# Edge sums of a graph network with the one-hots of half groups as the fixed operand, then copied, turned and added

## What is computed

```python
# layer 0: message = [nodes[src], edge] @ W, summed per receiver, then norm and a three-layer MLP
agg = segment_sum(concat([nodes[src], edge_attr_64], -1) @ W_message, dst)
h = layer_norm(relu(agg) + nodes);  nodes = layer_norm(nodes + relu_mlp_skip(h))
x = experts_0(x + ...)              # 16 experts, 2 of them per node
# layer 1: rows cut to their 32 largest entries, mean over the neighbours
x = x + segment_sum(sparse(x)[src], dst) / degree
x = experts_1(...)                  # 8 experts, 2 of them per node
```

## Time and profile before

| | us |
|---|---|
| median of 3 runs | 1449.61 (1449.51 to 1450.31) |
| span of the profiled execution | 1607.9 |
| setup | 0 to 40.6 |
| O0: groups, adjacency, node MLP | 40.6 to 558 |
| routing and experts of layer 0 | 558 to 865 |
| sparse rows | 865 to 1030 |
| O1: groups and neighbour means | 1030 to 1362 |
| routing, experts of layer 1, output | 1362 to 1608 |

### The profile page before, as it was taken

The page is one execution under the profiler, slowest core; times in us unless marked ns, Lnnn a source line. Parts: engine busy times, 40 slices in busy tenths (PEclk is TensorE's granted clock), DMA queues, the critical chain, the costliest instruction groups (busy, mean ns, idle before and its releaser), DMA issues. The chain is left out here.

```text
span 1607.9 us, 27179 instructions
## 1 busy us (share of the span) xinstructions
PE 1175.4 (73%) x7129; PEld 1007.4 (63%) x7130; DVE 709.5 (44%) x2376; ACT 661.1 (41%) x1842; POOL 746.3 (46%) x841
## 2 busy tenths in 40 slices
PE   1287788887899739999993777377778867478780
PEld 1277777876789628999992333166557666367670
DVE  7133455655446761111114999334433225522225
ACT  3554555654113333444443555576651002323230
POOL 5655555655550004222215776366456660266650
PEclk9977888877989958999996999755678885588885
DMA  5543344444440047999992232433223332422227
GB/s 173 147 112 107 107 109 115 118 114 105 112 115 25 17 160 254 350 352 352 349 322 85 85 89 72 132 90 95 76 76 103 97 94 70 133 78 78 81 75 249
DMA packets 186771, 220.03 MB, mean 137 GB/s; under 512 B 69103, under 2 KB 148503, under 8 KB 186382
## 3 DMA queue, kind: packets, MB, share of 16 engines
q1 hardware_dynamic: 148240, 125.81, 24.4%
q0 software_dynamic: 32352, 87.30, 18.7%
q10 hardware_dynamic: 6046, 5.40, 1.1%
HBM read 187.33 MB, written 32.19 MB: 137 GB/s over the span
## 5 line engine op out<-in xcount | busy, mean ns | idle before, releaser
L783 POOL DMA_INDIRECT O0G<-n_rows,src_tab x260 | 251.1, 966 | 194.5 <-PE O0ps_sums L802 91.8
L783 POOL DMA_INDIRECT O1G<-sparse_rows,src_tab x188 | 180.0, 958 | 125.9 <-issue 58.7
L802 PE MATMUL O0ps_sums<-O0OH,O0G 128*128 128x80 f32 x1040 | 160.1, 319 | 1.3 <-issue 1.2
L802 PEld LDWEIGHTS O0ps_sums<-O0OH,O0G 128*128 128x128 f32 x1040 | 153.7, 234 | 6.3 <-issue 2.7
L802 PEld LDWEIGHTS O1ps_sums<-O1OH,O1G 128*128 128x128 f32 x752 | 122.9, 251 | 14.1 <-issue 10.2
L1982 POOL DMA_INDIRECT e0xs<-token_rows,e0idx x60 | 56.8, 947 | 159.7 <-ACT e0idx L2071 155.9
L802 PE MATMUL O1ps_sums<-O1OH,O1G 128*128 128x80 f32 x752 | 123.3, 333 | 9.8 <-issue 7.4
L2027 PE MATMUL e0ps_h<-e0xT,e0W 128*128 128x128 f32 x1024 | 126.7, 277 | 0.8 <-ACT e0xT L2077 0.8
L2122 DVE TENSOR_TENSOR e0ys<-e0ps_y,NR 128x256 f32<-128x256 f32 x64 | 27.2, 425 | 215.3 <-PE e0ps_y L2041 215.3
L2027 PEld LDWEIGHTS e0ps_h<-e0xT,e0W 128*128 128x128 f32 x1024 | 121.1, 194 | 1.5 <-issue 1.4
L2041 PE MATMUL e0ps_y<-e0W,e0hidT 128*128 128x256 f32 x512 | 120.9, 379 | 0.0
(11 more groups left out here) (382 smaller groups left out, 2701.5 us busy)
## 6 DMA issues: line engine op xcount, KB each, us to landing
e0W<-in_L_ffn_w SPq DMA_DIRECT2D x128, 512.0 KB
O0EA<-in_edge_attr SPq DMA_DIRECT2D x97, 128.0 KB
expert_out<-e0ys SPq DMA_DIRECT2D x64, 128.0 KB
O0G<-n_rows,src_tab POOLq DMA_INDIRECT x260
e1W_all<-in_L_ffn_w SPq DMA_DIRECT2D x16, 256.0 KB, 6.0
n_rows<-NR SPq DMA_DIRECT2D x5, 640.0 KB
token_rows<-O0N SPq DMA_DIRECT2D x25, 128.0 KB
m0own<-token_rows SPq DMA_DIRECT2D x25, 128.0 KB
```

Of the source, the lines that this page charges most:

```text
L783: pool.indirect_dma_start(out=self.G[:, s, k, :], out_offset=None, in_=self.rows_dram, in_offset=bass.IndirectOffsetOnAxis(ap=src_tab[:, g ...
L802: last = nc.tensor.matmul(self.ps[o % 2][0:rows.shape[1], half * P:half * P + WINDOW], rows, self.OH[:, h, k, 0:WINDOW], start=(k == 0), s ...
```

## The change

The two operands of a gathered group's products change places. The one-hot of a tile (now 48 columns wide, relative to the base of its *half* group of two tiles) is the fixed operand; the gathered rows (256 columns) and the edge rows (65 columns) move. The first half's sums go to PSUM partitions 0 to 47, the second's to 64 to 111, in the order of tiles 0, 2, 1, 3. The result has nodes on the partitions, so it must be turned: ScalarE copies 112 x 321 (O1: 112 x 256) into SBUF (`copy`), TensorE turns it by three transposes (two in O1) into a third bank (`turn`, issued in the next slot before the products of the next group), and VectorE adds the two halves each at its own base (`add`, two value loads, two adds). Edges are dealt to tiles by 128 consecutive ones instead of every fourth, and the edge rows are loaded so too. Setup computes bases and relative places per half. To make room, the node stage's gate logits share a bank with another result (`ps_bg`, `ps_g`), with waits to match; small tables reuse `w_nodes` once it is no longer needed; `before` is made in `route`. The width of a group's window, which the order's safety limits use, goes from 80 to 88. The near groups and both adjacencies stay. Core of the diff:

```diff
-WINDOW = 80
+WINDOW = 88
+HALF_W = 48
+HALF_AT = 64
...
+rel_half = sb("rel_half", [P, NS, 2, GC // 2])
+base_half = sb("base_half", [1, NS, 2], I32)
...
-        for c in range(3):
-            last = nc.tensor.matmul(ps_e[0:1, c * P:c * P + NG], ends[:, c:c + 1], ident[0:NG, 0:NG], start=True, stop=True)
+        for c in range(5):
+            last = nc.tensor.matmul(ps_e[0:1, c * NG:(c + 1) * NG], ends[:, c:c + 1], ident[0:NG, 0:NG], start=True, stop=True)
         last.then_inc(s_rowp, 1)
         pe.wait_ge(s_row, 1)
-        nc.tensor.matmul(ps_b[:, 0:NG], ones[0:1, :], endr[0:1, 0, :], start=True, stop=True).then_inc(s_bb, 1)
+        nc.tensor.matmul(ps_b[:, 0:NG], ones[0:1, :], endr[0:1, 0, :], start=True, stop=True)
+        nc.tensor.matmul(ps_b[:, NG:3 * NG], ones[0:1, :], endr[0:1, 3:5, :].rearrange("a c g -> a (c g)"), start=True, stop=True).then_inc(s_bb, 1)
...
-                nc.vector.tensor_reduce(ends[:, 0:1], dlow[:], AX_X, ALU.min)
-                nc.vector.tensor_reduce(ends[:, 1:2], dstf[:], AX_X, ALU.max).then_inc(s_dv, 1)
+                nc.vector.tensor_reduce(ends[:, 3:5], dlow[:].rearrange("g (h e) -> g h e", h=2), AX_X, ALU.min)
+                nc.vector.tensor_reduce(half_top[:], dstf[:].rearrange("g (h e) -> g h e", h=2), AX_X, ALU.max).then_inc(s_dv, 1)
...
+                nc.vector.tensor_tensor(ends[:, 0:1], ends[:, 3:4], ends[:, 4:5], ALU.min)
+                nc.vector.tensor_tensor(half_span[:, 0, :], half_top[:], ends[:, 3:5], ALU.subtract).then_inc(s_dv, 1)
+                dve.wait_ge(s_dv, 6)
+                nc.vector.tensor_scalar(half_span[:, 1, :], ends[:, 3:5], ends[:, 0:1], float(2 * HALF_W - 1 - WINDOW), ALU.subtract, ALU.add).then_inc(s_dv, 1)
+                dve.wait_ge(s_dv, 7)
                 nc.vector.tensor_scalar(ends[:, 2:3], ends[:, 0:1], -1.0, MORE_TILE * P - 0.5, ALU.mult, ALU.add)
+                nc.vector.tensor_reduce(half_top[:, 0:1], half_span[:].rearrange("g k h -> g (k h)"), AX_X, ALU.max)
                 nc.vector.tensor_tensor(ends[:, 1:2], ends[:, 1:2], ends[:, 0:1], ALU.subtract).then_inc(s_dv, 1)
                 dve.wait_ge(s_dn, 5)
...
+        for h in range(2):
+            nc.vector.tensor_tensor(rel_half[:, :, h, :], rel_tab[:, DENSE_GROUPS:NG, 2 * h:2 * h + 2],
+                                    ps_b[:, (1 + h) * NG + DENSE_GROUPS:(2 + h) * NG].unsqueeze(2).to_broadcast([P, NS, 2]), ALU.subtract).then_inc(s_dv, 1)
...
+        hots, rows = HR * GC * HALF_W, 2 * self.row_cols
+        hot = sb(tag + "OH", [P, max(hots + rows, GU * GC * P)], F32, c)
+        self.OH = hot[:, 0:hots].rearrange("p (h c w) -> p h c w", h=HR, c=GC)
+        self.R = hot[:, hots:hots + rows].rearrange("p (r d) -> p r d", r=2)
         self.OH_any = hot[:, 0:GU * GC * P].rearrange("p (h c w) -> p h c w", h=GU, c=GC)
         self.ps = [pb(f"{tag}ps_sums{b}", [P, 512], c) for b in range(2)]
+        self.ps_turned = pb(tag + "ps_sums_turned", [P, 512], c)
+        self.adds_issued = 0
...
         for bank in self.ps:
-            nc.vector.memset(bank[P // 2:P, 2 * P:3 * P], 0.0)
+            nc.vector.memset(bank[:], 0.0)
+        nc.vector.memset(self.ps_turned[P // 2:P, 2 * P:3 * P], 0.0)
...
+        sp.dma_start(self.EA[:, s, 0:full, 0:DE], a["edge_attr_64"][g * GE:g * GE + full * P, :].rearrange("(c p) f -> p c f", p=P)).then_inc(self.edges_in[s], 16)
...
         if o >= 2:
-            pe.wait_ge(self.added, o - 1)
-        if n is not None:
-            for half in range(self.halves):
-                for k in range(GC):
-                    rows = self.EA[:, e, k, :] if half == 2 else self.G[:, r, k, half * P:(half + 1) * P]
-                    last = nc.tensor.matmul(self.ps[o % 2][0:rows.shape[1], half * P:half * P + WINDOW], rows, self.OH[:, h, k, 0:WINDOW],
-                                            start=(k == 0), stop=(k == GC - 1))
+            if self.is_gathered(o - 2):
+                pe.wait_ge(self.copied, self.gathered_before(o - 1))
+            else:
+                pe.wait_ge(self.added, self.adds_before(o - 1))
+        bank = self.ps[o % 2]
+        if self.is_gathered(o):
+            n = self.gathered_before(o)
+            pe.wait_ge(self.gathered[n % self.GR], (n // self.GR + 1) * 16 * GC)
+            for k in (0, 2, 1, 3):
+                at = k // 2 * HALF_AT
+                last = nc.tensor.matmul(bank[at:at + HALF_W, 0:D], self.OH[:, h, k, :], self.G[:, n % self.GR, k, :],
+                                        start=(k % 2 == 0), stop=(k % 2 == 1))
+            for k in (0, 2, 1, 3) if self.with_edges else ():
+                at = k // 2 * HALF_AT
+                last = nc.tensor.matmul(bank[at:at + HALF_W, D:D + DE + 1], self.OH[:, h, k, :], self.EA[:, e, k, :],
+                                        start=(k % 2 == 0), stop=(k % 2 == 1))
         else:
             for k in range(GC):
-                last = nc.tensor.matmul(self.ps[o % 2][0:DE + 1, 0:NARROW], self.EA[:, e, k, :], self.OH[:, h, k, 0:NARROW],
+                last = nc.tensor.matmul(bank[0:DE + 1, 0:NARROW], self.EA[:, e, k, :], self.OH[:, h, k, 0:NARROW],
                                         start=(k == 0), stop=(k == GC - 1))
         last.then_inc(self.summed, 1)
+
+    def copy(self, act, o):
+
+        if self.is_gathered(o):
+            n = self.gathered_before(o)
+            act.wait_ge(self.summed, o + 1)
+            if n >= 2:
+                act.wait_ge(self.turned, n - 1)
+            nc.scalar.activation(self.R[0:HALF_COLS, n % 2, :], self.ps[o % 2][0:HALF_COLS, 0:self.row_cols], ACT.Copy).then_inc(self.copied, 1)
+
+    def turn(self, pe, o):
+
+        if o >= 0 and self.is_gathered(o):
+            n = self.gathered_before(o)
+            pe.wait_ge(self.copied, n + 1)
+            if n >= 1:
+                pe.wait_ge(self.added, self.adds_before(self.plan.gathered[n - 1] + 1))
+            for part in range(self.halves):
+                cols = min(P, self.row_cols - part * P)
+                last = nc.tensor.transpose(self.ps_turned[0:cols, part * P:part * P + HALF_COLS], self.R[0:HALF_COLS, n % 2, part * P:part * P + cols],
+                                           ident[0:HALF_COLS, 0:HALF_COLS])
+            last.then_inc(self.turned, 1)
...
+        w, rel = (HALF_W, rel_half[:, g - DENSE_GROUPS, :, :].rearrange("p h c -> p (h c)")) if self.is_gathered(o) else (NARROW, rel_tab[:, g, :])
...
+        f = g - DENSE_GROUPS
+        bases = [dve.value_load(base_half[0:1, f, h:h + 1], min_val=0, max_val=NPAD) for h in range(2)]
+        dve.wait_ge(self.turned, self.gathered_before(o) + 1)
+        turned = self.ps_turned[:, 0:self.halves * P].rearrange("p (k w) -> p k w", k=self.halves)
+        for h in range(2):
+            self.add_window(dve, sumT[:, 0:self.halves, ds(bases[h], HALF_W)], turned[:, :, h * HALF_AT:h * HALF_AT + HALF_W])
+
+    def add_window(self, dve, window, sums):
+        if self.adds_issued:
+            dve.wait_ge(self.added, self.adds_issued)
         nc.vector.tensor_tensor(window, window, sums, ALU.add).then_inc(self.added, 1)
+        self.adds_issued += 1
...
                 for o in parts(groups_of(u), q):
+                    sums.turn(pe, o - 1)
                     sums.products(pe, o)
+                if u == plan.sum_steps and q == 0:
+                    sums.turn(pe, sums.groups - 1)
...
+                        for o in parts(groups_of(u), q):
+                            sums.copy(act, o)
...
+        self.ps_bg = self.ps_2[:, D:D + E0]
...
+            wait_tile(pe, S["logits_in"], t, 3)
...
-            wait_tile(pe, S["logits_in"], t, 1)
+            wait_tile(pe, S["z_ready"], t, -2)
...
+        self.ps_g = self.ps_n[:, D:D + E1]
```

163 lines of the change are left out of this document (90 added, 73 removed).

## The result

The changed kernel takes 1506.8 us (median of 4 runs, 1503.7 to 1509.1), the kernel before 1450.0 in the same comparison (4 runs, 1449.5 to 1451.1): a ratio of 1.039, 95% interval 1.037 to 1.041. It is **57 us slower**; 25 us less was forecast, and the result lies just over the upper end (1505) of the range given. The profiled execution of the change took 1503.7 us, with a span of 1502.0 us.

A forecast was written before the change was run, and what follows sets the result against it. The prediction took TensorE to bound the kernel, slowed by its clock and waits. Products -27, clock -15, new waits +12 and setup +2.5 made -27.5 us, scaled to -25: 1425 us, range 1390 to 1505.

The forecast's parts named there:

- So TensorE leads.: Bound of the group stretches: TensorE, busy for 82% of O0 and 73% of O1, more than any other engine.
- Overlap: TensorE's products: the halves overlap partly, 8 passes last as long as 5 (1.08 us), saving 40 us of TensorE.
- the rival of full overlap: TensorE's products on the two halves overlap fully: 1411 us, faster; chance 0.10.
- What reaches the end: Two thirds of TensorE's 40 us saving get past its waits to the end: -27 us.
- Clock, -15: TensorE's granted clock rises as the new passes stream 256 columns with no gap: -15 us, ends 0 and -35.
- New waits, +12: TensorE's turn waits for ScalarE's copy behind its one-hots, mostly at step ends: +12 us, bounds nothing or 44.
- Gate logits, nothing: Gate logits wait for `z_ready`, VectorE's add behind slot 2: hidden unless VectorE is late.
- VectorE's loads: VectorE's additional value load for a group runs ahead of the wait for the turn: at zero.
- Setup, +2.5: Setup gains nine or ten small VectorE instructions and four small passes: +2.5 us, ends 1 and 4.
- The copy's chain: Overlap holds, but copy, turn and two adds stand between products and next count at step ends: 1463 us; chance 0.15.
- No overlap: TensorE's eight passes of 256 columns follow each other: 1495 us, slower; chance 0.28.
- The scaling by 0.90: The summed -27.5 us on the profiled span of 1607.9 us was scaled by 1449.6/1607.9 to -25 us.

The follow-up runs named there:

- before_again: The kernel before, nothing edited, profiled a second time: 1447.2 us, span 1445.4 us.
- neither: The changed kernel with VectorE's `z_ready` add ahead of slot 2's adds, without copy and turns, with one add and one value load a group: 1400.4 us.
- turned, but unread, one add: Early third layer, but ScalarE copies an SBUF table, copies and turns run, and VectorE's one add a group (one load) reads the unturned bank: 1424.0 us.
- one add: Early third layer with copy and turn kept, but the second half's add and its value load left out: 1456.4 us.
- one load: Early third layer with both adds at the first half's base, so only the second value load is gone: 1466.4 us.
- early third layer: The changed kernel with VectorE's `z_ready` add, which reads the third layer, moved ahead of slot 2's adds: 1492.5 us.
- the last run: The kernel before with VectorE adding the adjacency's counts ahead of the group's sums in each slot: 1436.2 us, ratio 0.990.

## Why the prediction was wrong, point by point

The result is explained by these terms, each a difference of two measured times. Products: -50 us (1400.4 against 1450.2, with the setup's 2.4 us, the shared bank with its early add, and VectorE's narrower one-hots and adds inside). To that come, one after the other, copy and turn with VectorE not waiting for them +24, VectorE waiting +32, the second add +10, the second value load +26, the wait at the logits' shared bank +14: 1506.8. The order matters for the parts, since they are not independent. Copy and turn are worth 36 us with two adds and 56 with one, and the second add with its load the same; each pair alone takes 36 off, both together 92, as taking one delay out leaves the other. By stage:

| kernel | time, us | O0 | O1 |
|---|---|---|---|
| before (O0, O1 of `before_again`) | 1450.2 | 456.4 | 281.4 |
| neither | 1400.4 | 419.4 | 266.1 |
| turned, but unread, one add | 1424.0 | 429.8 | 278.8 |
| one add | 1456.4 | 459.2 | 278.9 |
| one load | 1466.4 | 468.1 | 281.2 |
| early third layer | 1492.5 | 490.8 | 286.2 |
| the change | 1506.8 | 502.7 | 288.7 |

VectorE's waiting for the turn (the fourth row against the third) costs 29 us in O0 and nothing in O1, and the second load (the sixth against the fifth) 23 and 5 us. O0 is where TensorE's next count waits for an add that stands behind the sums' adds.

- **"So TensorE leads."** This is the step that failed. The prediction had the loop before it and still gave VectorE's second add and value load "at zero, hidden by TensorE's products". The path goes through both engines by turns: adds, loads, count, products, adds. No engine covers another in it. VectorE's 55% busy (230 of 420 us) is no cover, since the time lies in waits and in loads that the busy time leaves out. Measured: 36 us with the turns in, 56 without.
- **Overlap.** "8 passes last as long as 5" was too small; they last as long as 4. Products and turns are 1.52 us a group in O0, with the changes of width inside, where 1.71 was written for full overlap, and 1.29 us in O1 where 1.36 was. So the rival of full overlap (0.10, 1411 us) was right on the products and 96 us off on the time. Of the two rules weighed, the Trainium skill, TensorEngine Tiling (Array Packing), Key Properties, with tiles that load and multiply in parallel, agrees with this case's trace (0.90 us for eight passes, where eight single ones are 1.73). The Trainium skill, TensorE: Matmul & The Clock Gate, What overlaps and what doesn't, with its strict program order, doesn't fit two halves: with the tiles in order, neighbours in the program share a half, and eight passes still take 0.90 us and start in pairs. The measurement decides.
- **What reaches the end.** "Two thirds" was too much even without the new work. The products alone save 2.32 - 1.23 = 1.09 us in 65 groups and 1.74 - 1.00 = 0.74 us in 47, 106 us of TensorE at full clock, and 50 at most reached the end. In O0 that kernel meets GpSimd's floor, which the prediction named (329 us for the gathers; 332 measured) and then didn't use.
- **Clock, -15.** It didn't come. Granted clock in O0 is 0.85 after and 0.94 before again; what the prediction took as room (0.83 to 1) was mostly that execution's own. No run shows a gain of clock from the new products: from 60 to 420 us the clock is 0.93 in the kernel with neither, 0.93 before again, and 0.82 with the change, where TensorE stands more.
- **New waits, +12.** The mechanism was partly right (in every second step the turn holds VectorE, the adjacency's adds behind it and TensorE's next count), its size wrong: +36 to +56 for copy and turn in place of 12, even over its upper end of 44 where VectorE is light. Its main carrier was wrong: TensorE's wait for the copy is 9.9 us, VectorE's for the turn 77.1 (for the products before, 41.0). And putting the copy first costs 17 us. GpSimd's wait for a buffer, which was to fall, rose from 35.0 to 90.2 us.
- **Gate logits, nothing.** 14 us came back when the add was moved forward; the wait was 22.7 us in ten places in the window shown. "Hidden unless VectorE is late" was the condition, and it is late.
- **VectorE's loads** were said to run "ahead of the wait for the turn", and so to be free. The second one cost 26 us, three quarters of the second add's price: a load is free only while VectorE would wait anyway, and in more than half of O0's groups it wouldn't (38 of 65, above).
- **Setup, +2.5.** Measured 2.4 (O0 starts at 39.4 us, before again at 37.0). Right in size.
- **Rivals.** The copy's chain (+13, 1463 us) was the right family, with a point of 1.5 us a step. It fell short as it had neither the second load nor the logits. "No overlap" gives 1495 us, near the result, for a reason that the trace excludes.
- **The range.** Its own range for the forecast, "with clock and waits at their ends", stops at 1450. With the ends that it names (clock 0, waits 44) the sum is -27 + 44 + 2.5 = +19.5, scaled +18, 1467 us.
- **The scaling by 0.90** took the first trace as a longer copy of a timed run. It wasn't: of the 162 us, 77 lay in O0, 48 in O1 and 34 in the experts of layer 1, and the other stages were within 4 us. In O0 the difference shows in TensorE's clock and in the waits for TensorE, which is just what the choice of bound rested on.

What stays open: how much of the 50 us is TensorE's and how much VectorE's lighter work; and how the 24 us (15 with two adds) of copy and turn that nobody on VectorE waits for divide between TensorE's passes (0.29 us a group in O0), its stand for the copy and ScalarE's 0.44 us a group.

## What to carry to other kernels

Where two engines hand work to each other several times in a step, price an edit by what it adds to the round trip (instructions, value loads and hops alike), not by who is busiest. Cheaper products are worth their saving only if the step that makes them cheap stays off the loop: here 50 us were won and 106 paid for turning, for a second base and for a shared bank. Look first at the order within the queue that the next engine waits for; putting the add that it waits for ahead was worth 14 us in the old kernel, for a few moved lines. And when the profiled span is 11% over the median of the timed runs, its waits and its clock aren't those of the kernel.

## What the runs showed of the hardware

- Float32 matmuls with fixed operands of 48 columns, with outputs at partitions 0 to 47 and 64 to 111, run two at a time: pairs of passes start 6 to 13 ns apart, and eight take 0.90 us at full clock in O0, whether the program alternates between the halves or not. The eight narrow passes behind them (65 columns) take 0.33 us with the halves alternating and 0.37 us without.
- Register loads on VectorE aren't in its busy time, but they take time in its queue. With two of them, VectorE was idle for 1.14 to 1.16 us between an add and the next (timeline of the change), and for 0.30 and 0.60 us where a one-hot ran just ahead of them (timeline of the last run). One more for each of the 112 groups cost 26 us of the total, against 10 us for the 112 adds that they serve.
